# All value projections moved from the attention stage into the preparing stage

## The reference, cut to what matters

```python
xn = (x - mean) / sqrt(var + 1e-5)
q, kv = xn @ Wq, xn @ Wkv                  # 256 -> 1024 and 2048
q, k = rope(q), rope(k)                    # turns the first 32 of 64 dims
attn = softmax(q @ k.T * 64 ** -0.5)       # per head, 1024 x 1024
attention = (attn @ v) @ Wout + bout
# quant: blocks of 16, scale = max|.| / 6, each value to the grid 0 .5 1 1.5 2 3 4 6
gate = quant(xn) @ quant(w_gate).T         # 256 -> 704
up = quant(xn) @ quant(w_up).T
ffn = quant(silu(gate) * up) @ quant(w_down).T
out = x + attention + ffn
```

## Time and profile before

| | us |
|---|---|
| median of 3 runs (range) | 2085.81 (2085.25 to 2088.85) |
| the profiled execution | 2086.47 |
| its span, first to last instruction | 2084.4 |
| stage 1, to 70.8 | 70.8 |
| stage 2, 70.8 to 393 | 322.2 |
| stage 3, 393 to 1968 | 1575 |
| stage 4, 1968 to 2084.4 | 116.4 |

### The profile page before, as it was taken

One profiled execution on the slowest core, in us unless ns is written; L12 is line 12 of the kernel. 1 busy time (PEld: TensorE's weight loads), 2 busy tenths in 40 slices (PEclk: granted clock), 3 DMA queues, 4 the chain that ended last, 5 costly groups with the idle time before them and its releaser, 6 DMA issues. The chain is left out here.

```text
span 2084.4 us, 30067 instructions
## 1 busy us (share of the span) xinstructions
PE 1888.5 (91%) x11300; PEld 1198.1 (57%) x11300; DVE 1556.3 (75%) x1967; ACT 826.0 (40%) x1068; POOL 1516.5 (73%) x699
## 2 busy tenths in 40 slices
PE   1288989669999999999999999999999999999499
PEld 0277888435555555555555555555555555555299
DVE  8699999467777777777777777777777777775154
ACT  1222332114444444444444444444444444444232
POOL 2356555218888888888888888888888888888444
PEclk9999999869999999999999999999999999999799
DMA  8100101300111121111112111111211111101286
GB/s 295 50 31 33 56 33 58 114 21 26 46 33 42 50 69 37 52 32 47 42 37 82 32 47 32 54 34 47 80 39 42 32 47 32 32 27 32 95 291 212
DMA packets 132282, 129.80 MB, mean 62 GB/s; under 512 B 40880, under 2 KB 96816, under 8 KB 132016
## 3 DMA queue, kind: packets, MB, share of 16 engines
q1 hardware_dynamic: 132144, 127.96, 19.4%
HBM read 87.56 MB, written 40.37 MB: 61 GB/s over the span
## 5 line engine op out<-in xcount | busy, mean ns | idle before, releaser
L1046 POOL TENSOR_TENSOR acc<-acc,prob 128x1024 f32<-128x1024 f32 x384 | 939.0, 2445 | 154.2 <-ACT prob L1089 125.8
L927 DVE TENSOR_REDUCE half_max<-m_ps 128x2 f32<-128x1024 f32 x512 | 625.4, 1221 | 340.2 <-PE m_ps L800 337.7
L1089 ACT ACTIVATE prob<-s_ps 128x1024 f32<-128x1024 f32 x512 | 498.4, 1025 | 362.0 <-PE s_ps L824 278.2
L839 PE MATMUL o_ps<-prob,v 128*64 128x512 f32 x2048 | 492.5, 602 | 0.0
L839 PEld LDWEIGHTS o_ps<-prob,v 128*64 128x64 f32 x2048 | 130.0, 136 | 250.8 <-issue 183.7
L1028 POOL TENSOR_TENSOR turned<-straight,shuffled 128x512 f32<-128x512 f32 x128 | 191.5, 1496 | 82.5 <-DVE shuffled L959 82.5
L800 PE MATMUL m_ps<-k_hi,q_hi 64*128 64x512 f32 x1024 | 233.3, 451 | 16.7 <-DVE half_max L927 14.4
L869 PE MATMUL misc_ps<-xT,wqk 128*128 128x512 f32 x768 | 219.2, 422 | 18.3 <-DMA xT<-xn_scratch 10.8
L869 PEld LDWEIGHTS misc_ps<-xT,wqk 128*128 128x128 f32 x768 | 138.9, 194 | 143.6 <-issue 109.0
L821 PE MATMUL s_ps<-q_hi,k_hi 64*128 64x512 f32 x1024 | 203.8, 393 | 0.0
L821 PE MATMUL s_ps<-q_lo,k_hi 64*128 64x512 f32 x1024 | 202.4, 390 | 0.0
(11 more groups left out here) (126 smaller groups left out, 2419.7 us busy)
## 6 DMA issues: line engine op xcount, KB each, us to landing
wqk<-wp_scratch SPq DMA_DIRECT2D x32, 512.0 KB, 4.1
inv_rows<-inv_scratch SPq DMA_DIRECT2D x128, 128.0 KB, 2.9
o_scratch<-o_norm SPq DMA_DIRECT2D x64, 256.0 KB, 2.0
o_in<-o_scratch SPq DMA_DIRECT2D x8, 2048.0 KB, 10.8
xn_scratch<-xnT SPq DMA_DIRECT2D x8, 1024.0 KB, 4.3
xT<-xn_scratch SPq DMA_DIRECT2D x8, 1024.0 KB, 5.8
wv<-wp_scratch SPq DMA_DIRECT2D x32, 256.0 KB, 3.5
wp_scratch<-wp_hl SPq DMA_DIRECT2D x8, 768.0 KB, 4.0
```

What stands on the lines that cost most here:

```text
L839: ins = nc.tensor.matmul(o_ps[head * DH:(head + 1) * DH, :], v[s // 2 % 2][:, kt, s % 2, at:at + DH], prob[n % SLOTS][:, head, :], start=k ...
L927: nc.vector.tensor_reduce(half_max[:, half % 2, :, t % GRP, part], m_ps[:, :, :], axis=AX.X, op=ALU.max, negate=True).then_inc(half_maxed, 1)
L1046: nc.gpsimd.tensor_tensor(acc[b][:, :, :], first, prob[n % SLOTS][:, :, :], ALU.add).then_inc(added, 1)
L1089: nc.scalar.activation(prob[n % SLOTS][:, :, :], s_ps[n % 2][:, :, :], ACT.Exp).then_inc(exp_done, 1)
```

## The change

The values of all heads and tiles are projected in the first stage, which is now called `prepare_part`, and not in the attention. That stage loads x first (four pieces), computes the statistics and the normalisation, and then for each of the 32 tiles: ScalarE normalises, TensorE turns, ScalarE and VectorE split, SyncE stores the split tile in `xn_scratch`, TensorE multiplies it with all 1024 value columns in 12 matmuls of 512 columns, ScalarE copies the result, SyncE stores it in `v_scratch` (512 KB a tile, two buffers). The value weights are loaded and split once (2048 columns). The quantisation of the three weights has one `low_x` of a tile behind each of its steps. The pairs' weights are q and k alone (`WP` 256 columns).

In the second stage the normalised tile is no longer turned, split or stored. In the attention `project_v`, `copy_v` and the loads of value weights go; each step loads its values (512 KB) from `v_scratch`. The q/k projections move to rounds 1, 3, 5 and 7, so the last one's rotary turn and split fall into rounds 0 and 1 of the next step.

```diff
-WP = 3 * P
+WP = 2 * P
...
+    CHUNK = TILES // 4
+    TURN_AT = {11: (0, 1), 22: (2, 3)}
+    HIGH_AT = {12: (0, 1), 23: (2, 3)}
+    PAIR_AT = {1 + 3 * pr: pr for pr in range(PAIRS)}
...
+            def store_xT(t):
+                sp.wait_ge(t_low, t + 1)
+                sp.dma_start(io["xn_scratch"][t], xT[t % 4][:, :, :, :].rearrange("p h c n -> p (h c n)").bitcast(F32)).then_inc(xT_stored[t % 4], 16)
+            def store_v(t):
+                sp.wait_ge(v_copied, 2 * t + 2)
+                sp.dma_start(io["v_scratch"][t], v_out[t % 2][:, :]).then_inc(v_stored[t % 2], 16)
...
+            sp.dma_start(ident[:, :], io["tables"][:, 0:P]).then_inc(tables_in, 16)
+            for k in range(4):
+                sp.dma_start(x_all[:, k * CHUNK * D:(k + 1) * CHUNK * D].rearrange("p (t d) -> p t d", d=D),
+                             io["x"][k * CHUNK * P:(k + 1) * CHUNK * P, :].rearrange("(t p) d -> p t d", p=P)).then_inc(x_in[k], 16)
+            sp.dma_start(wv_in[:, :], io["wv"]).then_inc(wv_loaded, 16)
...
-            for pr in range(PAIRS):
-                u = pr % 2
-                if pr >= 2:
-                    sp.wait_ge(wp_low, pr - 1)
-                sp.dma_start(wp_in[:, u, :], io["w_pairs"][pr]).then_inc(wp_loaded[u], 16)
-                if pr >= 1:
-                    sp.wait_ge(wp_low, pr)
-                    sp.dma_start(io["wp_scratch"][pr - 1], wp_hl[:, 1 - u, :, :].bitcast(F32)).then_inc(wp_stored[1 - u], 16)
-            sp.wait_ge(wp_low, PAIRS)
-            sp.dma_start(io["wp_scratch"][PAIRS - 1], wp_hl[:, 1, :, :].bitcast(F32)).then_inc(wp_stored[1], 16)
+            for t in range(TILES):
+                store_xT(t)
+                if t:
+                    store_v(t - 1)
+                if t - 1 in PAIR_AT:
+                    pr = PAIR_AT[t - 1]
+                    sp.wait_ge(wp_low, pr + 1)
+                    sp.dma_start(io["wp_scratch"][pr], wp_hl[:, pr % 2, :, :].bitcast(F32)).then_inc(wp_stored[pr % 2], 16)
+                    if pr + 2 < PAIRS:
+                        load_pair(pr + 2)
+            store_v(TILES - 1)
             for u in range(2):
                 sp.wait_ge(wp_stored[u], 16 * PAIRS // 2)
-            sp.wait_ge(tables_in, 16)
+                sp.wait_ge(v_stored[u], 16 * TILES // 2)
+            for u in range(4):
+                sp.wait_ge(xT_stored[u], 16 * TILES // 4)
...
+            def low_x(t):
+                dve.wait_ge(t_high, t + 1)
+                nc.vector.tensor_tensor(xT[t % 4][:, LO, :, :], xt_ps[t % 2][:, 0:D].rearrange("p (c n) -> p c n", c=DC),
+                                        xT[t % 4][:, HI, :, :].bitcast(F32), ALU.subtract).then_inc(t_low, 1)
...
-            beside = [lambda k=k: statistics(k) for k in range(TILES // GRP)]
-            for w in range(2):
-                dve.wait_ge(w_ff_in[w], 32)
-                block_scales(nc, chain, w_in[:, w, :], tmp)
-                round_blocks(nc, chain, w_in[:, w, :], wq8[:, w, :], tmp).then_inc(quantised, 1)
-                if w == 1:
...
-            dve.wait_ge(w_ff_in[2], 16)
-            block_scales(nc, chain, wd_in[:, :], tmp, beside[0:4])
-            low_parts(2)
-            low_parts(3)
-            round_blocks(nc, chain, wd_in[:, :], wd8[:, :], tmp, beside[4:8]).then_inc(quantised, 1)
...
+            low_x(0)
+            low_x(1)
+            dve.wait_ge(pads, 2)
+            LINKS = SCALE_OPS + 5
+            for w in range(3):
+                src, dst = (w_in[:, w, :], wq8[:, w, :]) if w < 2 else (wd_in[:, :], wd8[:, :])
+                dve.wait_ge(w_ff_in[w], 32 if w < 2 else 16)
+                beside = [lambda t=2 + LINKS * w + k: low_x(t) for k in range(LINKS)]
+                block_scales(nc, chain, src, tmp, beside[0:SCALE_OPS])
+                if w:
+                    low_parts(2 * w - 2)
+                    low_parts(2 * w - 1)
+                round_blocks(nc, chain, src, dst, tmp, beside[SCALE_OPS:]).then_inc(quantised, 1)
+            for t in range(2 + 3 * LINKS, TILES):
+                low_x(t)
...
+                if t >= 2:
+                    act.wait_ge(t_turned, t - 1)
+                nc.scalar.activation(xn[t % 2][:, :], x_all[:, t * D:(t + 1) * D], ACT.Identity,
+                                     bias=kept["shift"][:, t:t + 1], scale=rstd[:, t:t + 1]).then_inc(t_normed, 1)
+            def high_x(t):
+                act.wait_ge(t_turned, t + 1)
+                if t >= 4:
+                    act.wait_ge(xT_stored[t % 4], 16 * (t // 4))
+                nc.scalar.activation(xT[t % 4][:, HI, :, :], xt_ps[t % 2][:, 0:D].rearrange("p (c n) -> p c n", c=DC),
+                                     ACT.Copy).then_inc(t_high, 1)
+            def copy_v(t, k):
+                act.wait_ge(v_mult, 2 * t + k + 1)
+                if k == 0 and t >= 2:
+                    act.wait_ge(v_stored[t % 2], 16 * (t // 2))
+                nc.scalar.activation(v_out[t % 2][:, k * 512:(k + 1) * 512], v_ps[k][:, :], ACT.Copy).then_inc(v_copied, 1)
+            act.wait_ge(wv_loaded, 16)
+            nc.scalar.activation(wv[:, HI, :], wv_in[:, :], ACT.Copy).then_inc(wv_high, 1)
+            act.wait_ge(var_ready, 1)
+            nc.scalar.activation(ln[4][:, :], ln[3][:, :], ACT.Sqrt).then_inc(sd_ready, 1)
+            act.wait_ge(ln_ready, 1)
+            normalise(0)
+            normalise(1)
+            normalise(2)
+            high_x(0)
+            high_x(1)
+            for t in range(TILES):
+                if t + 3 < TILES:
+                    normalise(t + 3)
+                if t + 2 < TILES:
+                    high_x(t + 2)
+                copy_v(t, 0)
+                if t in PAIR_AT:
+                    high_pair(PAIR_AT[t])
+                copy_v(t, 1)
+                for n in HIGH_AT.get(t, ()):
                     high_parts(n)
...
+                if t == TILES - 5:
+                    act.wait_ge(wo_loaded, 16)
+                    nc.scalar.activation(wo[:, HI, :], wo_in[:, :], ACT.Copy).then_inc(wo_high, 1)
...
+            def turn_x(t):
+                pe.wait_ge(t_normed, t + 1)
+                if t >= 2:
+                    pe.wait_ge(t_low, t - 1)
+                for c in range(DC):
+                    ins = nc.tensor.transpose(xt_ps[t % 2][:, c * P:(c + 1) * P], xn[t % 2][:, c * P:(c + 1) * P], ident[:, :])
+                ins.then_inc(t_turned, 1)
+            def project_v(t):
+                pe.wait_ge(t_low, t + 1)
+                for k in range(2):
+                    if t:
+                        pe.wait_ge(v_copied, 2 * t + k - 1)
+                    i = 0
+                    for xs, ws in PARTS:
+                        for c in range(DC):
+                            ins = nc.tensor.matmul(v_ps[k][:, :], xT[t % 4][:, xs, c, :],
+                                                   wv[:, ws, c * INNER + k * 512:c * INNER + (k + 1) * 512],
+                                                   start=i == 0, stop=i == 3 * DC - 1)
+                            i += 1
+                    ins.then_inc(v_mult, 1)
+            def turn_w(n):
+                kind, w, c = units[n]
                 pe.wait_ge(quantised, w + 1 if kind == "gu" else 3)
-                if n >= 2:
+                if 2 <= n < 5:
                     pe.wait_ge(low_out, n - 1)
...
+            pe.wait_ge(tables_in, 16)
+            turn_x(0)
+            turn_x(1)
+            pe.wait_ge(wv_ready, 1)
+            for t in range(TILES):
+                if t + 2 < TILES:
+                    turn_x(t + 2)
+                project_v(t)
+                for n in TURN_AT.get(t, ()):
+                    turn_w(n)
+            for n in range(4, len(units)):
+                turn_w(n)
...
-                        for i in range(2):
-                            low_x(n + GRP, t, i)
+                        low_x(n + GRP, t)
...
-CHUNK_ROUND = {1: K0, 2: K1, 3: Q0, 5: Q1}
+CHUNK_ROUND = {1: K0, 3: K1, 5: Q0, 7: Q1}
...
-            def project_v(s, k):
-                begin("v", s, k)
-                group = s // 2
-                if s % 2 == 0 and k == 0:
-                    pe.wait_ge(wv_loaded[group % 2], 32 * (group // 2 + 1))
-                for j in range(2):
-                    t = 4 * (s % 2) + 2 * k + j
-                    n = 0
-                    for xs, ws in PARTS:
-                        for c in range(DC):
-                            ins = nc.tensor.matmul(misc_ps[:, j * 2 * P:(j + 1) * 2 * P], xT[:, t, xs, c, :],
-                                                   wv[group % 2][:, ws, c, :, :].rearrange("p a n -> p (a n)"),
-                                                   start=n == 0, stop=n == 3 * DC - 1)
-                            n += 1
...
-                    if r >= 6 and scoring(s + 2):
-                        project_v(s + 2, r - 6)
...
+                    if r == 0 and scoring(s + 1):
+                        rotate(s + 1, Q1)
...
+                    if r == 1 and scoring(s + 1):
```

(17 more changed lines are left out.)

157 lines of the change are left out of this document (60 added, 97 removed).

## The result

| | before | after |
|---|---|---|
| median (range) of 4 runs, us | 2085.87 (2085.25 to 2088.85) | 2106.47 (2105.29 to 2107.45) |
| ratio, 95% interval | | 1.0096 (1.0078 to 1.0113) |
| span of the profiled execution | 2084.4 | 2104.7 |
| stage 1 | 70.9 | 141.1 |
| stage 2 | 322.4 | 318.5 |

Forecast were 2096 us and slower; the sign holds, the loss is 20.6 us where 10 were worked out. By the spans, stage 1 adds 70.2 us (forecast 76), stage 2 gives 3.9 (7.5), the attention 45.9 (58). Three errors of 5.8, 3.6 and 12.1 us: the first helped, the other two cost, and the attention's is the largest.

The account below looks back on a forecast made before the run. TensorE was taken to bound stage 3 (VectorE in rounds without projections), VectorE stage 2, and TensorE the changed stage 1. 2084.4 + 76 - 58 - 7.5 = 2094.9 us, adjusted to a 2096 us median; range 2074 to 2115.

Parts of the forecast that it names:

- Stage 1, +76: Preparing stage becomes a line on TensorE: 147 us, 76 more than 70.8 (64 to 95).
- stall 5.2: Stage 1 after tile 23: TensorE waits 5.2 us as VectorE's low part stands behind two of turned weights.
- The 0.2 for late stores: Stage 1: 0.2 us added to each of 24 tiles for value stores queued behind the weight pairs' transfers.
- Stage 2, -7.5: Second stage: 4 us from the tiles (0 to 9.5), the rest waited out behind GpSimd, and 3.5 from its lead.
- Attention, -58: Stage 3: step 46.97 to 45.2 us, 53 over 30 steps (39 to 71), plus 5.6 in the lead.
- the size of `o_norm`: Attention, round 1: `o_norm` takes 1.7 us after 2.2 for `low`, making the next reduction 0.3 us late.
- The faster rival: Attention: `low` and `o_norm` do not fall behind GpSimd, a step is 44.6 and the time 2079 us; chance 0.25.
- Round 4's 0.40 us: Attention, round without projection: VectorE's reduction, turn, reduction take 4.77 us where TensorE could leave after 4.37.
- The lead: Start of the attention: fourth projection and two value blocks go, a turn comes later; saves 5.6 us (3 to 8).
- GpSimd's share: Attention: GpSimd's busy share rises from 82% to 89% of a step, an argument against the faster rival.
- GpSimd as the bound: Rival, attention: GpSimd stretched by 15%, step 46.3, saving 0.7, time 2128 us; chance 0.03.
- DMA as stage 1's bound: Rival: value stores late in all first 24 tiles, a tile 4.0 us instead of 3.35, +16, 2112 us; chance 0.12.

Follow-up runs that it names:

- experiment 8: Changed kernel with projections in rounds 1, 2, 3 and 5 again and the third and fourth weight block turned behind tile 20: 2057.4 us, ratio 0.9866.
- experiment 11: On experiment 8, the last 4 of the 12 matmuls that make a tile's values left out: 2048.8 us, ratio 0.9814.
- experiment 2: Changed kernel with the first `o_norm` of a step moved from round 1 to behind the second reduction of round 2: 2075.0 us, ratio 0.9941.
- experiments 9 and 12: Shuffle of the rotary turn put behind its round's second reduction: on experiment 8, 2055.6 us (9); on the kernel before, 2083.5 us (12).

## Why the prediction was right in sign and short by half

- **Stage 1, +76, measured +70.2.** The mechanism and its parts were right: start 27.0 (27.5), the first tile's slow clock 2.8 (2.2), turns of weights 2.6 (2 x 1.3), stall 5.2 (5.22), end 3.9 (3.9). The 1.2 of slow clock behind the stall was in no term. The term that was mis-sized is the tile: 24 x 3.35 + 8 x 3.15 = 105.6 us were put down, 32 x 3.00 = 96 came, and some 2.4 in single waits. The 0.2 for late stores was not due: ScalarE waited for stores three times in all, 2.0 us. A store landed in 2.9 us, as estimated.
- **The Trainium skill, "DMA: Bandwidth & Descriptors", section "Where 436 GB/s comes from"**, had the HBM limit at about 358 GB/s, above the demand, and spoke against the 0.2. The trace agrees that the 0.2 wasn't due. As a ceiling the figure doesn't hold here: at the start of stage 3 the kernel before loads 365 GB/s between 396 and 404 us, and 401 in the last 6 us of them. For stage 1's mixture of loads and stores the room is smaller all the same: between 60 and 100 us experiment 8 moved 332 GB/s, and experiment 11, in which stores do become late, 322.
- **The quantisation is hidden** behind TensorE, as forecast, except for that stall.
- **Stage 2, -7.5, measured -3.9.** The lead's 3.5 were nearly right (the first `h` comes 2.9 us earlier in the stage). Of the tiles' 9.5 I gave 4 and 0.2 came. The step was right in kind, "VectorE waits out what it gained", and too timid in size.
- **Attention, -58, measured -45.9.** The step that failed is the size of `o_norm`: "3.8 + 2.2 + 1.7 = 7.7, where the next reduction was due at 6.8 + 0.55 = 7.35; 0.3 us late". In round 1 `q_lo` took 1.84 and `o_norm` 2.89, not 2.2 and 1.7, and the reduction came 0.96 us late, with no slack in round 2. The forecast bounds for both instructions together were 0 to 1.0, and 0.6 was taken; the upper end was right. 44.6 + 0.96 = 45.56 is nearly the step seen (45.61). That is 0.4 a step, 12 of the 15 us that are missing between the turns of the maxima. The last such interval, of a step without projections, also grew, from 42.2 to 43.4 us; the rest isn't located. The 1.71 us of the earlier trace rows was a lone wait behind the rest of one addition; behind `q_lo`, which itself ends only when GpSimd's first addition is over, `o_norm` meets the whole of the second. In round 6, where up to 0.6 was feared, it took 0.84 and cost nothing. The sign doesn't hang on luck; that the time came no further from the forecast does, since stage 1's shorter tiles took 5.8 us back. Without them the loss would have been 26.
- **The faster rival's mechanism** is experiment 2: with the waits gone, a step is 44.7 (44.6 forecast) and the time 2075 (2079 forecast). It had been given 0.25.
- **Round 4's 0.40 us** was read wrongly: "TensorE could leave it at 917.69" leaves out the turn of the maxima that starts there. TensorE's own length of it is 4.64 us, as experiments 9 and 12 show. The changed kernel's sum didn't rest on it, since 4.77 stood there before and after.
- **The lead**, 5.6 forecast, gave 7.75; why it gave 2 us more isn't worked out.
- **GpSimd's share**, "from 82% to 89%", set a mean of the stage against the sum of a step. By step it was 40.2 / 46.97 = 86% before, so the rise that spoke against the faster rival was 3 points and not 7.
- **GpSimd as the bound** did not come: its additions went from 2.445 to 2.47 us in the mean. DMA as stage 1's bound did not come, but experiment 11 shows it to be one step away.

## What to carry to other kernels

Work that is moved out of a full stage into one with room costs there what does not fit beside what is already done; here 92 us of TensorE's busy time left the attention and 98 came into stage 1, which grew by 70. The rest of the result was decided by order alone: one two-operand VectorE instruction, moved by one round, was worth 31 us, more than the whole loss. So behind each such instruction write down which GpSimd instruction runs at its start, and whether VectorE has slack before the next engine waits; a gain in VectorE's work counts only as far as it is not waited out there.
